# A four-layer graph kernel: the last layer opens with eight diagonal units, each beside one of the third layer's last eight tiles

## The chip, the cores and the metric

The kernel runs on one core of a Trainium2 chip. Its engines are TensorE (PE, matmuls), VectorE (DVE), ScalarE (ACT), GpSimd (POOL) and SyncE (SP, which here starts the transfers). Each works through its own queue in order and waits on semaphores for the others. The metric is the device time of one execution in microseconds (us), the median of several runs.

## The reference

Four graph layers on 4096 nodes with 64 features each share one 4096 x 4096 adjacency. After each layer the rows are normalised. The change touches the end of the third layer and the fourth.

```python
def _L0_gnn_ref(x, L, weight):             # layer 1: Chebyshev terms of L @ x
    ...
def _L1_gnn_ref(h, node_adj, edge_adj, ...):   # layer 2: attention and gates
    ...
def _L2_gnn_ref(input, adj, weight, bias):     # layer 3
    support = input @ weight
    mask = (adj != 0).astype(support.dtype)
    rank = jnp.cumsum(mask, axis=1)
    # at most the last 100 neighbours of a row count, each with a decay by its rank;
    # the decays times support are summed over the row
    ...
# layer 4 (curvature 1): pairs of nodes x, y, both moved with _expmap
sub = _mobius_add(-x, y, c)
sub_norm = jnp.maximum(jnp.linalg.norm(sub, axis=-1, keepdims=True), MIN_NORM)
2.0 / (sqrt_c * lam_x) * jnp.arctanh(arg) * sub / sub_norm   # _logmap
# the log maps are weighted by adj, summed over the neighbours and mapped back
```

The distance between two nodes is symmetric. So the fourth layer computes g, a factor made of the distance of a pair, once for both directions.

## The kernel before

**Third layer.** It works on 32 tiles of 512 x 1024 adjacency entries, `decayed(i)` on TensorE (L892 and L898, 16 matmuls of 512 columns). For each tile the rank codes come back from DRAM as bytes and are turned into decays in four blocks: two by ScalarE (L1287), one by VectorE (L1901), one by GpSimd (L615). Two buffers hold decays. The table `L2_TILES` gives the order; quarter Q of the nodes is done with its last tile. Then `copy_sums2`, `fold_sums`, `read_sums2`, `row_spread`, `root2` and `scale2` turn the sums of a quarter into normalised rows and the columns of U, the nodes' extended rows. `turn_nodes` transposes U, and `copy_nodes` puts it as UT and VT where the distances are computed from. `move_x` (L985) multiplies a quarter of the nodes with the layer's weights, `keep_moved` copies the result.

**Fourth layer.** It works on 80 units. A unit is one block of 128 nodes against a quarter of 1024 nodes. 32 units are on the diagonal of quarters (D, `own_units`), 48 off it (O, `off_units`). Per unit:
- TensorE: `distances` (L958), and, after VectorE's `multiply`, `push_apart` (L971);
- ScalarE: five passes over 128 x 1024: `raise_dist` (L1373), Ln (L1386), Exp (L1393), Exp (L1397), Ln (L1381);
- VectorE: `multiply` (L2015), the sum (L2099) and g (L2092); for O twice `mirror_weights` (L2025) as well;
- GpSimd: g times the edges (L635);
- TensorE: `gather` (L1012); for O also `turn_g` twice, four transposes each (L998), and per four O units, a quad, eight pairs of mirror products (L1027).

The order of every queue is written out by hand as a loop over "periods" n. TensorE's queue in period n is: push n, distances n+1, the second turn of g n-2, gather n-2, the mirror products that `products` plans for n (two behind two O units, otherwise one, three in the first quad), the first turn of g n-1. Distances n+1 wait for sum n-1, because two sets of PSUM banks alternate. The kind of each unit is set by the string "OODOD". `MOVED_AT`, `ROWS_AT`, `LAST_AT` and `POINTS_AT` say in which period the pieces of the third layer's end are done. Only tile 31 is still open when unit 0 has been pushed.

## Time and profile before

| | us |
|---|---|
| median of 3 runs | 1735.33 (1733.4 to 1735.41) |
| profiled execution | 1742.45, span 1740.6 |
| PE busy | 1542.5 |
| DVE busy | 1250.4 |
| ACT busy | 947.7 |
| POOL busy | 297.3 |

The span runs from the first to the last instruction of the profiled execution. Busy times are over the whole span; the stages have different limits, and the fourth layer is only the last 520 us of it. There ScalarE, which is 54% busy over the whole, is at nine tenths for most slices. The granted TensorE clock has a mean of 0.948 of full speed; it is low at the start of the fourth layer.

### The profile page before, as it was taken

The numbers are of one execution on the slowest core, as the hardware profiler recorded it, in microseconds if no ns is written. First come the engines' busy times: TensorE is split into PE (matmuls) and PEld (weight loads), VectorE is DVE, ScalarE is ACT, GpSimd is POOL, SyncE is SP. The second block draws the span as 40 slices with busy tenths as digits, with TensorE's granted clock in tenths as the row PEclk, the third lists the DMA queues.
The fourth block names the chain that finished last, engine by engine and source line by source line (L and its number), as shares of the span: only waits on it lengthen the run. The fifth ranks groups of instructions, "written<-read, shape, count | busy, mean of one in ns | idle before, by whom it ended". The sixth has DMA issues, their size and how long they took to land.

```text
span 1740.6 us, 21314 instructions
## 1 busy us (share of the span) xinstructions
PE 1542.5 (89%) x8169; PEld 653.1 (38%) x8214; DVE 1250.4 (72%) x1609; ACT 947.7 (54%) x920; POOL 297.3 (17%) x150
## 2 busy tenths in 40 slices
PE   6999989999999699999999997788788888888880
PEld 1433333333333344444444444233333333333330
DVE  4677699986888656747749654456567888888877
ACT  1233477753344433324343344656567999999964
POOL 1000000000000000000000002675224444444430
PEclk9999999999999799999999998999678999999995
DMA  9999599938999335333334302346124444544410
GB/s 349 412 413 413 213 357 381 392 130 316 413 413 381 115 146 193 147 146 146 145 135 156 145 1 73 121 133 218 37 97 133 148 155 136 186 163 158 136 46 24
DMA packets 118109, 348.99 MB, mean 201 GB/s; under 512 B 6324, under 2 KB 31224, under 8 KB 117752
## 3 DMA queue, kind: packets, MB, share of 16 engines
q1 hardware_dynamic: 106784, 329.27, 50.9%
q10 hardware_dynamic: 11224, 18.36, 2.8%
q8 instruction: 66, 1.08, 0.3%
q14 instruction: 35, 0.29, 0.1%
HBM read 329.78 MB, written 17.83 MB: 200 GB/s over the span
## 4 chain that ended last, share of the span: by engine, by line
PE 52%; issue 18%; DVE 13%; POOL 13%; ACT 2%; DMA 2%; SPq 0%; POOLq 0%; DVEq 0%; ACTq 0%
PE ps L741 13%; PE ps L863 13%; POOL ring L635 11%; PE ps L869 9%; DVE work L1611 4%; PE ps L674 3%; DVE work L1648 3%; PE ps L673 3%; PE ps L892 2%; POOL work L615 2%; PE ps L808 2%; DMA ring<-in_adjT 2%; PE ps L705 1%; PE ps L898 1%; DVE work L1624 1%
## 5 line engine op out<-in xcount | busy, mean ns | idle before, releaser
L615 POOL TENSOR_SCALAR work<-work 128x1024 int16<-128x1024 uint8 x32 | 97.0, 3041 | 1106.2 <-DMA work<-codes 1044.5
L863 PE MATMUL ps<-ring,X 128*64 128x512 f32 x512 | 264.0, 597 | 13.3 <-DVE ring L1867 13.3
L1134 ACT ACTIVATE work<-ps,code_bias 128x1024 uint8<-128x1024 f32 x128 | 135.8, 1111 | 247.7 <-PE ps L674 239.2
L864 PE MATMUL ps<-work,X 128*64 128x512 f32 x512 | 264.0, 597 | 0.0
L1255 ACT ACTIVATE work<-ring 128x2048 f32<-128x2048 f32 x64 | 122.2, 1911 | 222.0 <-PE ps L871 201.1
L635 POOL TENSOR_TENSOR ring<-ring,work 128x1024 f32<-128x1024 f32 x80 | 189.8, 2372 | 280.8 <-DVE work L2092 280.6
L871 PE MATMUL ps<-work 128*64 128x512 bf16 x768 | 208.2, 380 | 0.0
L869 PE MATMUL ps<-work 128*64 128x512 bf16 x768 | 208.2, 380 | 0.0
L958 PE MATMUL ps<-work 96*128 96x512 f32 x320 | 169.5, 655 | 0.0
L741 PE MATMUL ps<-ring,work 128*64 128x512 f32 x704 | 161.7, 601 | 0.0
L1864 DVE TENSOR_SCALAR work<-ring 128x2048 bf16<-128x2048 f32 x64 | 78.5, 1226 | 106.0 <-PE ps L871 105.8
L869 PEld LDWEIGHTS ps<-work 128*64 128x64 bf16 x768 | 84.8, 110 | 177.8 <-issue 152.3
L2099 DVE SCALAR_TENSOR_TENSOR work<-ps,work 128x1024 f32<-128x1024 f32 x80 | 97.9, 1224 | 46.5 <-ACT work L1393 34.4
L1638 DVE TENSOR_TENSOR work<-work 128x512 bf16<-128x512 bf16 x248 | 105.4, 425 | 33.3 <-DVE work L1611 12.9
L1867 DVE TENSOR_SCALAR ring<-ring 128x2048 f32<-128x2048 f32 x64 | 78.1, 1220 | 40.7 <-ACT work L1255 40.7
L1611 DVE TENSOR_TENSOR work<-work,ring 128x1024 f32<-128x1024 f32 x85 | 103.5, 1218 | 0.7
L741 PE MATMUL ps<-ring,X 128*64 128x512 f32 x352 | 88.0, 646 | 16.5 <-DMA ring<-in_adjT 16.5
L674 PE MATMUL ps<-work,minus_ones 128*128 128x512 bf16 x256 | 98.0, 383 | 4.7 <-DVE Y L1591 2.5
L892 PE MATMUL ps<-work 128*128 128x512 bf16 x243 | 67.0, 416 | 29.6 <-ACT work L1287 13.3
L1012 PE MATMUL ps<-ring 128*64 128x512 f32 x320 | 89.3, 637 | 2.9 <-POOL ring L635 2.9
L863 PEld LDWEIGHTS ps<-ring,X 128*64 128x64 f32 x512 | 68.9, 137 | 55.7 <-issue 16.0
L1287 ACT ACTIVATE work<-work 128x2048 int16<-128x2048 uint8 (+1 forms) x32 | 67.5, 2119 | 39.0 <-PE ps L898 36.6
(316 smaller groups left out, 2766.0 us busy)
## 6 DMA issues: line engine op xcount, KB each, us to landing
ring<-in_adjT SPq DMA_DIRECT2D x90, 2048.0 KB, 10.6
work<-in_adjT SPq DMA_DIRECT2D x26, 2048.0 KB, 12.0
ring<-in_adjT SPq DMA_DIRECT2D x48, 1024.0 KB, 7.7
codes<-work ACTq DMA_DIRECT2D x64, 256.0 KB, 6.1
work<-codes SPq DMA_DIRECT2D x32, 512.0 KB, 3.6
ring<-in_adjT SPq DMA_DIRECT2D x32, 512.0 KB, 3.6
X<-in_x ACTq DMA_DIRECT2D x1, 1024.0 KB, 6.9
work<-in_xT SPq DMA_DIRECT2D x2, 512.0 KB, 22.6
```

Source lines behind the costliest of these rows:

```text
L615: nc.gpsimd.tensor_scalar(decay[i % 2][:, 3, :].rearrange("p (h c) -> p h c", h=2), code_in[:, i % RING, :, 3, :], 128.0, None, ALU.mult). ...
L635: nc.gpsimd.tensor_tensor(u.edges, u.edges, u.angle, ALU.mult).then_inc(weighted, 1)
L674: mm = nc.tensor.matmul(ps[:, bank, :], minus_ones[:], later[:, u, j, :], start=False, stop=True)
L741: mm = nc.tensor.matmul(ps[i * F:(i + 1) * F, a.banks + h, :], rows_of(a, k), a.room[:, k, cols], start=start, stop=stop)
L863: nc.tensor.matmul(ps[0:F, h, :], rows, ring[:, r, k, cols], start=start, stop=stop)
L864: nc.tensor.matmul(ps[F:P, h, :], rows, negs[:, pair, i, cols], start=start, stop=stop)
L869: nc.tensor.matmul(ps[0:F, 2 + h, :], part, more[:, pair, i, cols], start=start and t == 0, stop=stop and t == 2)
L871: mm = nc.tensor.matmul(ps[F:P, 2 + h, :], part, less[:, pair, i, cols], start=start and t == 0, stop=stop and t == 2)
L958: mm = nc.tensor.matmul(ps[:, u.banks + h, :], UT[:, u.rows * P:(u.rows + 1) * P], VT[:, cols], start=True, stop=True)
L1134: nc.scalar.activation(codes[:, u, k:k + 2, :].rearrange("p k c -> p (k c)"), ps[:, bank:bank + 2, :].rearrange("p k c -> p (k c)"), ACT.Relu,
L1255: nc.scalar.activation(negs[:, pair], ring[:, s % RING, 2 * pair:2 * pair + 2, :], ACT.Relu, scale=-1.0).then_inc(negs_made, 1)
L1611: ins = V.tensor_tensor(row_sum[:, a.q, :], row_sum[:, a.q, :], edges, ALU.add)
```

## The change

The unit order becomes eight D, then 22 times OOD, then OOOODD. `JOINT = 8`, and `BEFORE = SLOTS - JOINT` is 24: unit 0's distances are put in front of tile 24, and period n holds tile 25+n behind distances n+1. The decays of these tiles are made inside the periods by all three engines. Of the nodes only quarter 0 is turned as a whole before the units; quarters 1, 2 and 3 follow as halves (`turn_half`, `copy_half`, `copy_signs`) in the periods that `HALVES_AT` names. GpSimd copies their signs, which ScalarE did for quarters 1 and 2. Rows are scaled in four groups, one for each quarter, and no longer in three. `move_x` moves from periods 2, 3, 4, 10 to 10, 11, 12, 16. The first units' angles and edges get other places in the ring, loaded between code tiles 11 and 12.

```diff
-        sums2_in = [turn_in[:]] * 3 + [x_moved_words[:, 0:QC]]
+        sums2_in = [turn_in[:], turn_in[:], x_moved_words[:, QC:2 * QC], x_moved_words[:, 0:QC]]
...
+        JOINT = 8
...
-                self.angle = angles[:, n % 3, :]
+                self.angle = ring[:, 3, n % 3, :] if n < JOINT else angles[:, n % 3, :]
...
-        for five in range(UNITS // 5):
-            for kind in "OODOD" if five < UNITS // 5 - 1 else "OOODD":
...
+        for kind in "D" * JOINT + "OOD" * 22 + "OOOODD":
...
+        AHEAD = 7
+        for u in own_units[0:AHEAD]:
+            u.edges = (ring[:, 2, 0, :], ring[:, 2, 1, :], ring[:, 2, 2, :], ring[:, 2, 3, :], ring[:, 1, 0, :],
+                       ring[:, 1, 1, :], ring[:, 3, 3, :])[u.place]
...
-        COPIED = (1, 2, 3, 5)
-        MOVED_AT = (2, 3, 4, 10)
-        ROWS_AT = 4
-        LAST_AT = 6
-        POINTS_AT = [1, 8, 11]
+        COPIED = (1, 3, 5, 7)
+        SIGNED = (2, 6, 10, 14)
+        HALVES_AT = {3: (1, 0), 4: (1, 1), 7: (2, 0), 8: (2, 1), 14: (3, 0), 15: (3, 1)}
+        HALF_BANKS = (None, 4, 4, 7)
+        MOVED_AT = (10, 11, 12, 16)
+        ROWS_AT = 10
+        POINTS_AT = [6, 9, 14]
...
-        SUM_AT, READ_AT, SPREAD_AT = (15, 17, 25), (17, 19, 27), (18, 20, 28)
-        TURN_AT, OUT_AT = (22, 23, 30), (24, 25)
+        SUM_AT, READ_AT, SPREAD_AT = (15, 17), (17, 21), (18, 22)
+        ROOT_AT, SCALE_AT, OUT_AT = 19, 20, 22
...
-        GROUPS = ((0, 1), (2,), (3,))
-        ROOT_AT, SCALE_AT = (21, 29), (22, 30)
+        BEFORE = SLOTS - JOINT
...
+            for i in range(BEFORE + 3):
+                make_decays(i)
             for u in units:
+                if BEFORE + 3 + u.n < SLOTS:
+                    make_decays(BEFORE + 3 + u.n)
                 pool.wait_ge(g_made, u.n + 1)
...
+            def turn_half(n, h):
+
+                pe.wait_ge(ext_ready, n + 1)
+                wait_for_copies(COPIED[n - 1] + h)
+                if h == 0 and n == 1:
+                    pe.wait_ge(sum2_read, 3)
+                if h == 0 and n == 3:
+                    pe.wait_ge(moved_kept, 3)
                 for c in range(GB):
...
+            for i in range(12, BEFORE + 1):
+                if i == BEFORE:
+                    distances(units[0])
                 decayed(i)
...
             for n in range(LAST_PERIOD):
+                if n in HALVES_AT:
+                    turn_half(*HALVES_AT[n])
                 if unit_at(n):
                     push_apart(units[n])
                 if unit_at(n + 1):
                     distances(units[n + 1])
+                if BEFORE + 1 + n < SLOTS:
+                    decayed(BEFORE + 1 + n)
...
-                if n == 0:
-                    decayed(SLOTS - 1)
                 if n == 1:
-                    fold_sums(NQ - 1)
+                    fold_sums(2)
+                if n == JOINT:
+                    fold_sums(3)
...
+            def copy_half(n, h):
+
+                act.wait_ge(vt_copied, COPIED[n - 1] + h + 1)
...
                 if n == 0:
-                    copy_sums2(NQ - 1)
+                    copy_sums2(2)
                 if n == 1:
-                    copy_nodes(2)
-                    read_sums2(NQ - 1)
+                    scale2(1)
                 if n == 2:
-                    row_spread(2, NQ - 1)
+                    read_sums2(2)
                 if n == 3:
+                    row_spread(2, 2)
+                if n == 5:
+                    scale2(2)
+                if n == JOINT - 1:
+                    copy_sums2(3)
+                if n == JOINT:
                     dve.wait_ge(decay_used, SLOTS)
                     V.memset(aggT[:], 0.0).then_inc(sums_cleared, 1)
-                if n == 5:
-                    scale2(2)
+                if n == 9:
+                    read_sums2(3)
+                if n == 10:
+                    row_spread(2, 3)
+                if n == 12:
+                    scale2(3)
```

The first place is TensorE's queue where the units begin. Before, this is period 0 with tile 31 (L892, L898), between push (L971) and distances (L958) of units 0, 1 and 2:

```order
L971 MATMUL ps<-work 128x512 [waits prod_made,signs_copied]
L971 MATMUL ps<-work 128x512
L958 MATMUL ps<-work 128x512 x2
L892 MATMUL ps<-work 128x512 [waits decay_pool,decay_dve,decay_act,part2_made2]
L892 MATMUL ps<-work 128x512 x7
L898 MATMUL ps<-work 64x512 x8
L971 MATMUL ps<-work 128x512 [waits prod_made]
L971 MATMUL ps<-work 128x512
L958 MATMUL ps<-work 128x512 [waits vt_tail_copied,sum_made,vt_copied,ut_copied]
L958 MATMUL ps<-work 128x512
```

Now it is the end of period 2 and period 3: a gather (L1041), half of quarter 1's nodes turned (L962), push (L1000), distances (L989), a tile (L920, L926) and the next gather:

```order
L1041 MATMUL ps<-ring 64x512 [waits sum2_copied,points_made,weighted]
L1041 MATMUL ps<-ring 64x512
L962 MATMUL ps<-ident,work 128x128 [waits vt_tail_copied,vt_copied,sum2_read,ut_copied,ext_ready]
L962 MATMUL ps<-ident,work 128x128 x3
L1000 MATMUL ps<-work 128x512 [waits prod_made]
L1000 MATMUL ps<-work 128x512
L989 MATMUL ps<-work 128x512 [waits sum_made]
L989 MATMUL ps<-work 128x512
L920 MATMUL ps<-work 128x512 [waits decay_pool,decay_dve,decay_act,part2_made2]
L920 MATMUL ps<-work 128x512 x7
L926 MATMUL ps<-work 64x512 x8
L1041 MATMUL ps<-ring 64x512 [waits points_made,weighted]
```

A tile stands behind the distances in seven periods, where it stood in one, and the turn of half a quarter stands in front of a push.

The second place is VectorE's queue in period 10 of the new kernel, behind the points: the sum of the first eight units (L2075), g 9 (L2125), mirror multiplies (L2058), sum 10 (L2132), multiply 11 (L2048), the end of the spread (L1858 to L1860) and the norm of rows (L1558):

```order
L2075 TENSOR_TENSOR work<-work,ps 128x512 [waits sums_cleared,gathered]
L2125 SCALAR_TENSOR_TENSOR work<-work,stage_words 128x1024 [waits inv_made,angle_made]
L2058 TENSOR_TENSOR work<-ps,ring 128x4x128 [waits strip_in0,g_turned]
L2132 SCALAR_TENSOR_TENSOR work<-ps,work 128x1024 [waits far_added,root_made]
L2048 SCALAR_TENSOR_TENSOR turn_in<-ps,turn_in 128x1024 [waits raised]
L1858 TENSOR_TENSOR room_f<-Y 128x512
L1859 TENSOR_REDUCE stats<-room_f 128x8 [waits row_steps2]
L1860 TENSOR_SCALAR stats<-stats 128x8 [waits row_steps2]
L1558 TENSOR_TENSOR X<-Y,stats 128x512
L2058 TENSOR_TENSOR work<-ps,ring 128x4x128 [waits g_turned]
```

Before, the same pieces stood in period 2, where there was no sum of units to add yet and no norm of rows:

```order
L2092 SCALAR_TENSOR_TENSOR work<-work 128x1024 [waits inv_made,angle_made]
L2025 TENSOR_TENSOR work<-ps,ring 128x4x128 [waits strip_in0,g_turned]
L2099 SCALAR_TENSOR_TENSOR work<-ps,work 128x1024 [waits far_added,root_made]
L2015 SCALAR_TENSOR_TENSOR stage_words<-ps,stage_words 128x1024 [waits raised]
L1822 TENSOR_TENSOR room_f<-Y 128x512
L1823 TENSOR_REDUCE stats<-room_f 128x8 [waits row_steps2]
L1824 TENSOR_SCALAR stats<-stats 128x8 [waits row_steps2]
L2025 TENSOR_TENSOR work<-ps,ring 128x4x128 [waits g_turned]
L2092 SCALAR_TENSOR_TENSOR work<-work,turn_in 128x1024 [waits inv_made,angle_made]
```

The last mirror multiply of the pair, which the next turn of g and move_x wait for, has two instructions more ahead of it, and the spread's two halves are one period apart as they were.

## Rows read from the trace of the kernel before

**Rows 1.** Windows, start-up and rhythm: length, busy us (count) by engine, clock, DMA.

```profile
1215.00:1358.00 143.00, 116.13 (x403) 53.28 (x404) 97.51 (x131) 96.35 (x102) 45.39 (x21) 0.79 0.29 94
1358.00:1680.00 322.00, 285.59 (x1206) 114.41 (x1206) 268.89 (x271) 297.80 (x306) 144.89 (x61) 1.00 0.46 150
```

**Rows 2.** Source view of L971: duration min/median/max, first and last start.

```profile
L971 PE MATMUL ps<-work x160: 371/380/629, 1215.0 to 1680.3; 3*128 3x512 bf16 x160
```

**Rows 3.** Timeline of one cycle: start, us, engine, instructions [idle before <- releaser].

```profile
1421.32 0.60 PE L971 MATMUL ps<-work 3*128 3x512 bf16 x2 [0.59 <-DVE stage_words L2015]
...
1426.22 0.60 PE L971 MATMUL ps<-work 3*128 3x512 bf16 x2 [0.51 <-DVE work L2015]
...
1431.35 0.60 PE L971 MATMUL ps<-work 3*128 3x512 bf16 x2 [0.58 <-DVE turn_in L2015]
...
1431.88 1.98 PE L958 MATMUL ps<-work 96*128 96x512 f32 x4
...
1434.98 1.21 DVE L2015 SCALAR_TENSOR_TENSOR stage_words<-ps,stage_words 128x1024 f32<-128x1024 f32 x1
...
1436.93 0.63 PE L998 MATMUL ps<-ident,work 128*128 128x128 f32 x4 [0.76 <-DVE work L2025]
...
1437.49 0.60 PE L971 MATMUL ps<-work 3*128 3x512 bf16 x2
...
1440.04 1.02 ACT L1373 ACTIVATE work<-ps 128x1024 f32<-128x1024 f32 x1 [1.10 <-PE ps L958]
```

**Rows 4.** Timeline of PE: last tiles and start-up.

```profile
1135.10 3.59 PE L892 MATMUL ps<-work 128*128 128x512 bf16 x8 [5.99 <-ACT work L1245]
...
1183.78 1.67 PE L892 MATMUL ps<-work 128*128 128x512 bf16 x7
...
1234.56 1.11 PE L998 MATMUL ps<-ident,work 128*128 128x128 f32 x4 [5.65 <-DVE work L2025]
...
1240.35 3.68 PE L985 MATMUL ps<-w_sb,work 64*128 64x64 f32 x16
...
1244.92 3.78 PE L958 MATMUL ps<-work 96*128 96x512 f32 x4
...
1265.68 3.20 PE L985 MATMUL ps<-w_sb,work 64*128 64x64 f32 x16 [1.61 <-DVE work L2057]
...
1302.59 0.60 PE L971 MATMUL ps<-work 3*128 3x512 bf16 x2 [0.21 <-DVE stage_words L2015]
...
1358.60 0.60 PE L971 MATMUL ps<-work 3*128 3x512 bf16 x2
```

**Rows 5.** Timeline of DVE: scalings and reading of sums.

```profile
1205.77 0.99 DVE L1928 SCALAR_TENSOR_TENSOR stats<-stats 128x8 f32<-128x8 f32 x1
...
1212.47 0.69 DVE L1948 TENSOR_TENSOR work<-Y,stats 128x512 f32<-128x512 f32 x1
...
1227.32 0.67 DVE L1965 TENSOR_TENSOR Y<-ps,Y 128x512 f32<-128x512 f32 x1
...
1229.67 0.69 DVE L1815 TENSOR_TENSOR Y<-Y,stats 128x512 f32<-128x512 f32 x1
...
1275.79 0.16 DVE L1928 SCALAR_TENSOR_TENSOR stats<-stats 128x8 f32<-128x8 f32 x1
...
1279.51 0.69 DVE L1948 TENSOR_TENSOR work<-Y,stats 128x512 f32<-128x512 f32 x1
```

**Rows 6.** Timeline of ACT: decays of a tile, copy of half a quarter.

```profile
1204.79 1.91 ACT L1287 ACTIVATE work<-work 128x2048 int16<-128x2048 uint8 x1 [0.56 <-PE ps L898]
...
1293.75 0.59 ACT L1364 ACTIVATE work<-ps 96x512 f32<-96x512 f32 x1 [1.54 <-DVE work L1960]
```

**Rows 7.** Page, costliest groups: count | busy us, mean ns | idle before.

```profile
L615 POOL TENSOR_SCALAR work<-work 128x1024 int16<-128x1024 uint8 x32 | 97.0, 3041 | 1106.2 <-DMA work<-codes 1044.5
...
L635 POOL TENSOR_TENSOR ring<-ring,work 128x1024 f32<-128x1024 f32 x80 | 189.8, 2372 | 280.8 <-DVE work L2092 280.6
```

More of the change, by code:

```diff
@@ L213, in adjacency_stack @@
         units, off_units, own_units = [], [], []
-        for five in range(UNITS // 5):
-            for kind in "OODOD" if five < UNITS // 5 - 1 else "OOODD":
-                left, stream = (off_left, off_units) if kind == "O" else (own_left, own_units)
-                u = Unit(len(units), *left.pop(0))
-                u.place = len(stream)
-                stream.append(u)
-                units.append(u)
+        for kind in "D" * JOINT + "OOD" * 22 + "OOOODD":
+            left, stream = (off_left, off_units) if kind == "O" else (own_left, own_units)
+            u = Unit(len(units), *left.pop(0))
+            u.place = len(stream)
+            stream.append(u)
+            units.append(u)
+        assert len(units) == UNITS
         for stream in (off_units, own_units):
@@ L392, in adjacency_stack @@
         edges_in = [[sem(f"edges_in{i}_{r}") for r in range(2)] for i in range(2)]
+        first_edges_in = [sem(f"first_edges_in{i}") for i in range(AHEAD)]
         strip_in = [sem(f"strip_in{r}") for r in range(2)]
@@ L532, in load_own @@
                     "p a b c -> p (a b c)")
-                sp.dma_start(u.edges, src).then_inc(edges_in[1][u.place % 2], 16)
+                sp.dma_start(u.edges, src).then_inc(
+                    first_edges_in[u.place] if u.place < AHEAD else edges_in[1][u.place % 2], 16)
             def load_strip(quad):
@@ L542, in load_strip @@
                     sp.dma_start(strip_part(quad, t), src).then_inc(strip_in[quad % 2], 16)
-            sp.wait_ge(pair_used, 2 + 2 * (SLOTS - RING + 2))
-            for u in own_units[0:2]:
+            for i in range(12):
+                load_codes(i)
+            for u in own_units[0:AHEAD]:
                 load_own(u)
@@ L548, in _ @@
                 load_off(u)
[L549 to L552 removed]
+            for i in range(12, SLOTS):
+                load_codes(i)
+            turns = [(own_units[i - 2].n + 1, 0, i) for i in range(AHEAD, len(own_units))]
+            turns += [(4, 3, 0), (AHEAD, 4, 1)]
             turns += [(off_units[i - 3].n + 1, 1, i) for i in range(4, len(off_units), 2)]
@@ L561, in _ @@
                     load_off(off_units[i])
+                if kind >= 3:
+                    sp.wait_ge(gathered, done)
+                if kind == 4:
+                    sp.wait_ge(weighted, JOINT)
+                if kind >= 3:
+                    load_strip(i)
                 if kind == 2:
@@ L607, in _, with make_decays @@
             pool.sem_inc(consts_made, 1)
-            for i in range(SLOTS):
+            def make_decays(i):
                 pool.wait_ge(code_loaded[i % RING], (i // RING + 1) * 16)
@@ L1350, in _ @@
             part2(3, 2)
-            for i in range(14, SLOTS):
+            for i in range(14, BEFORE + 2):
                 make_decays(i)
@@ L1996, in _ @@
             rest2(3, 1)
-            for i in range(14, SLOTS):
+            for i in range(14, BEFORE + 2):
                 make_decays(i)
```

174 lines of the change are left out of this document (84 added, 90 removed).

## The prediction

> **How the profile was read.** First the windows view, which cuts the run's end into stages. From the first push (the matmuls of L971, the first own step of a unit) at 1215.0 us, the last layer takes 143 us to reach push 18 and then 322 us to push 79 [rows 1, 2, 4]. In the second stretch ScalarE is busy 297.8 of 322 us at full TensorE clock, so it nearly sets the pace; in the first no engine is full (TensorE 116, ScalarE 96 of 143 us) and the granted clock is 0.79 [rows 1]. So the end of the run is 18 units of start-up, 61 units of rhythm, and a tail after the last push that the change leaves alone.
>
> Then the timeline of one cycle of the rhythm. I call "period n" the time from push n to push n+1. TensorE's work in it depends on whether units n-1 and n-2 are off the diagonal (O) or on it (D), since only O units have transposes (turn_g) and mirror products. The pushes at 1421.32, 1426.22, 1431.35 and 1437.49 give 4.90 us for a period behind D and O, 5.13 behind O and D, and 6.14 behind two O [rows 3]. In the last one TensorE does 8 transposes and two mirror products; it waits 0.76 us for VectorE's mirror multiply, pushes late, and ScalarE then sits 1.10 us until the distances come [rows 3]. Nothing gives this back.
>
> Last the start-up. Extra TensorE and VectorE pieces (move_x, the sums' folding and reading, scaling, the nodes' copies) stand in the period's chain. After a wait of 5.65 us for a VectorE multiply, move_x takes 3.68 us and a unit's distances 3.78 us against 1.98 us in the rhythm; that is 1.2 GHz against 2.4. A wait of only 1.61 us is again followed by a slow move_x (3.20 us) [rows 3, 4].
>
> The sum is made on the profiled execution (1742.45 us, span 1740.6), and its difference is put on the median of the runs, 1735.33, which lies 7.1 us lower.
>
> **Rhythm (units 18 to 79).** The order changes from OODOD to OOD. Periods 18 to 78 are 61. Before: 13 behind two O, 24 behind O and D, 24 behind D and O: 13 x 6.14 + 24 x 5.13 + 24 x 4.90 = 320.5 us; measured 1680.3 - 1358.6 = 321.7 [rows 2, 4], so 1.2 us are left over for starts of a quad. Now two D lead out and OOD has one pair of O in three: 22 behind two O (19 in the cycles, 3 in the closing OOOODD), 20 and 19 of the others: 22 x 6.14 + 20 x 5.13 + 19 x 4.90 = 330.8, with the same 1.2 it is 332.0. **Cost +10.3 us.** Each kind of period in this sum occurs in the old cycle beside the same neighbours, and the planner gives each the same number of mirror products (two behind two O, else one), so I take it as it stands. Bounds: +5 if a pair's delay is partly hidden by ScalarE's slack, +14 if the three pairs in a row at the end add to each other.
>
> **Entry.** Tile 24 starts at 1183.78; its first matmuls (seven records) take 1.67 us [rows 4], the whole some 2.7. Until there the new order has one turn of nodes fewer on TensorE, and the scaling is for one quarter; but the first scaling still holds up a turn. I leave tile 24 where it was. Push 0 comes behind it: the raised distances (1.02 us) and the multiply (1.21 us) [rows 3] go on beside the tile, and ScalarE has two decay instructions (1.91 us each) [rows 6] in front. I get 4.8 us, so push 0 at 1188.6, 26.4 us earlier than before.
>
> **Periods 0 to 7, beside tiles 25 to 31.** ScalarE has 297.8/61 = 4.9 us for a unit [rows 1] and 1.9 for a tile's decays, so 6.8 us; TensorE has a tile (2.7), distances, push and gather, 6.2 us; GpSimd 3.04 + 2.37 = 5.4 us [rows 7]. The floor is 6.8, set by ScalarE. On top comes what stands in the chain, laid out by hand in the order of each queue:
> - 0: no Ln yet, 5.3. 1: copy_sums2 and root2, 7.6.
> - 2: scale2(1) is in VectorE's queue ahead of g 1, sum 2, multiply 3 and read_sums2, and turn_half(1,0) waits for the sums read. TensorE has about 4 us with nothing and holds push 3 back: 11.3.
> - 3: the clock is low after this gap: distances 3.8, the tile slower; VectorE's decays and row_spread stand ahead of copy_half, ScalarE's two copies (0.59 each, [rows 6]) behind it, and turn_half(1,1) behind these: 12.5. 4: gap before it again: 9.8.
> - 5: 6.4. 6: scale2(2) again ahead of multiply 7: 8.0. 7: copy_sums2 and copy_half before turn_half(2,1): 8.5.
> Together 69.4, so push 8 at 1258. Before, push 8 is at 1302.6 [rows 4]: a lead of 44.6 us, at the widest.
>
> The second and the third scaling of before (19 instructions, L1928 to L1948) show both prices: 7.4 us with GpSimd running beside it, 4.4 us with it idle [rows 5]. I take 4.7 in periods 1 and 5, since GpSimd then waits for g. The Trainium skill (GPSIMD Engine Reference, section 8. Key points) says that GpSimd shares its SBUF interfaces with VectorE and contends with instructions of two SBUF inputs or in a 2-port mode. The two durations agree; by the rule alone both scalings would run beside decays in this stage, at 7.4 us, and the sum would be 5 to 6 us higher.
>
> **Periods 8 to 17.** Nearly everything that before stood in periods 1 to 10 beside units 1 to 10 now stands here beside units 8 to 17:
> - 8: turn_half(2,1), fold_sums(3), aggT cleared: 8.4. 9: 7.6.
> - 10: VectorE's queue is read_sums2 (3.0 us, from 1227.32 to 1230.36 [rows 5]), points, the sum of the first eight units, g 9, a mirror multiply, sum 10, multiply 11, spread, norm rows, and only then the mirror multiply that turn_g 9 waits for; behind it move_x(0) at 3.7 us: 16.2.
> - 11: distances 3.8, raise, multiply, norm, keep_moved, move_x(1): 12.1. 12: the same with scale2(3) in front of keep_moved: 16.2.
> - 13 and 14: turn_half(3,0) and (3,1) behind keep_moved and the copies: 11.5 and 10.8. 15: 6.5. 16: move_x(3): 8.5. 17: 5.2.
> Together 103.0: push 18 at 1361.0, 2.4 us later than before. The 44.6 us of lead are given back, since the ten periods cost about twice those of the rhythm. DMA is not in the sum: 5.5 MB of edges are issued between code tiles 11 and 12, where TensorE waits 5.99 us for another copy anyway [rows 4], and each ring place is loaded again as many units ahead as before. The new waits on copied signs and half nodes are in the terms above; what is queued behind them is push n.
>
> Bounds of the start-up: if every stretch that I put at 1.2 GHz ran at 2.4, seven periods lose 2.3 us each on distances and push, six turns 0.4, three move_x 1.8: -24 us. If both scalings run beside GpSimd and tile and unit are slow in all eight joint periods, about +14 us.
>
> **Sum:** +2.4 + 10.3 = +12.7 us: 1755 for the profiled execution, **1748 us** for the median.
>
> **Rivals.**
> - A, the lead is kept (faster). Mechanism: in periods 2 to 8 the tiles' matmuls lie between distances and gather and keep TensorE at 2.4 GHz, so move_x and distances run at 1.98 instead of 3.8 us. -24 + 12.7 gives -11: 1724 us. For it: granted clock near full in most of the tile stage. Against it: here a wait of 1.61 us was enough. It decides if push 18 comes before 1345. Chance 0.18. The skill (TensorE: Matmul & The Clock Gate, section Loop structure matters more than you think) says that matmuls which follow each other at once hold the clock while VectorE copies; by this rule the joint stage would be such a loop, and the time would be this rival's.
> - B, the rhythm is not slower: the 6.14 us belong to something in the five-cycle that three-cycles lack. Then +2.4: 1738 us. Against it: the wait for the mirror multiply comes with the two O before it, always. Chance 0.13.
> - C, the joint stage costs more: GpSimd's decays for tile 27+n are queued behind weighting n-1, which waits for g, and VectorE's scalings run beside it; 2 us in each of eight periods: +29, 1764 us. For it: in the tile stage of before TensorE already waits for GpSimd's decays. Against: 5.4 us fit into 8. Chance 0.19.
> - Forecast, 0.50, own range 1740 to 1757.
>
> **The numbers.** A change under 0.2% (3.5 us) can't be told from none. Faster: A and a little of the forecast's lower edge, 0.20. Same: most of B and a little of the forecast, 0.13. Slower: the rest, 0.67. The range 1727 to 1763 reaches to near A and takes most of C.
>
> **What will show it.** Right: periods of 6.14 us once in three units at a granted clock of 1.00, 16.2 us a cycle; push 0 near 1189, push 8 near 1258, push 18 near 1361; GpSimd, ScalarE and VectorE none full in the start-up; long periods 2, 3, 10, 11, 12. Wrong: a cycle under 15.9 us; a granted clock over 0.9 between push 8 and push 18; or push 8 later than 1270 with TensorE waiting for L635's decays (C).

## The result and the profile after

The changed kernel takes 1756.92 us (median of 4 runs, 1753.96 to 1760.57), the kernel before 1735.04 beside it: a ratio of 1.0129 with an interval of 1.0105 to 1.0153, or 22 us slower. The forecast was 1748, slower, with a range of 1727 to 1763. The direction holds, the time is inside the range, and of the 22 us the forecast had 12.7.

The profiled execution of the changed kernel took 1754.72 us (span 1753.0). A second profile of the unchanged kernel (the first experiment) took 1735.18 (span 1733.4), 7.3 us less than the one that the forecast was made from. It is the fairer one to compare with. The stages, from the pushes (L971 before, L1000 after):

| us | push 0 at | pushes 0 to 18 | pushes 18 to 79 | tail | span |
|---|---|---|---|---|---|
| before, as in the rows | 1215.0 | 143.5 | 321.5 | 60.5 | 1740.6 |
| before, profiled again | 1211.6 | 139.7 | 321.5 | 60.6 | 1733.4 |
| after | 1184.6 | 178.4 | 331.4 | 58.7 | 1753.0 |
| after less before again | -27.0 | +38.7 | +9.9 | -1.9 | +19.6 |

Windows of the kernel after, for the joint stage (pushes 0 to 8), units 8 to 17 and the rhythm; the columns are the window, its length, busy us by engine (count), the granted clock, the DMA share and GB/s. They answer to [rows 1].

```profile
1184.60:1254.80 70.20, 59.66 (x217) 22.67 (x218) 48.55 (x85) 55.75 (x59) 36.99 (x17) 0.81 0.17 56
1254.80:1363.00 108.20, 83.12 (x238) 38.99 (x238) 62.29 (x92) 52.97 (x58) 32.12 (x18) 0.65 0.24 78
1363.00:1694.30 331.30, 294.42 (x1290) 122.18 (x1290) 276.06 (x282) 299.21 (x307) 144.69 (x61) 1.00 0.46 153
```

The same view of the kernel before, profiled again:

```profile
1211.60:1291.60 80.00, 61.16 (x193) 29.86 (x193) 49.87 (x73) 44.82 (x49) 16.49 (x7) 0.70 0.16 51
1291.60:1351.30 59.70, 52.65 (x218) 21.68 (x218) 48.13 (x58) 52.23 (x54) 28.95 (x14) 0.94 0.49 159
1351.30:1672.80 321.50, 285.09 (x1203) 113.97 (x1203) 268.43 (x271) 297.27 (x306) 144.94 (x61) 1.00 0.46 150
```

Single profiles of one stage differ by some us, and the experiments show by how much. In the eight profiles of the changed kernel and its variants push 0 lies between 1182.9 and 1190.0, though their edits touch nothing ahead of it but one instruction that makes zeros. Experiment 3 leaves the first 18 periods of the changed kernel as they are too, and they take 174.7 us there, with 67.1 for pushes 0 to 8 at a granted clock of 0.89. So a difference of 3 or 4 us between two profiles of the start-up shows nothing by itself.

TensorE's first two windows add up to 142.8 busy of 178.4 us after and 113.8 of 139.7 before: 29.0 more busy and 9.7 more idle. Seven tiles stand in the stretch where one stood (tile 31, behind push 0), so six have come into it. Their matmuls (L920 and L926; before, L892 and L898) are busy for 24.1 us after and 2.9 before: 21 us more, of which six tiles are 16 at the forecast's own estimate of 2.7 us each at full clock. The distances of the 18 units take 11 us more with the same instructions (54.6 and 43.4), since of them 11 took over 2.5 us after (most 3.78, full clock 1.98), and 5 before. I call these slow distances from here on. The turns, gathers and mirror products differ by smaller amounts of either sign. So the 27 us by which the units start earlier are spent on the tiles brought with them, on half clock and on waits, and more comes on top.

The rhythm, in the timeline of PE (start, us, engine, instructions, idle before and its releaser); it answers to [rows 3]:

```profile
1422.43 0.63 PE L1026 MATMUL ps<-ident,work 128*128 128x128 f32 x4 [0.77 <-DVE work L2058]
1422.98 0.60 PE L1000 MATMUL ps<-work 3*128 3x512 bf16 x2
...
1427.88 0.60 PE L1000 MATMUL ps<-work 3*128 3x512 bf16 x2 [0.50 <-DVE stage_words L2048]
...
1433.02 0.60 PE L1000 MATMUL ps<-work 3*128 3x512 bf16 x2 [0.60 <-DVE work L2048]
...
1438.61 0.63 PE L1026 MATMUL ps<-ident,work 128*128 128x128 f32 x4 [0.76 <-DVE work L2058]
1439.17 0.60 PE L1000 MATMUL ps<-work 3*128 3x512 bf16 x2
```

4.90, 5.14 and 6.15 us, a cycle of 16.2; the wait of 0.76 for VectorE's mirror multiply stands ahead of the late push, as before. The waits view sums it up: 22 such waits, where the order has 22 pairs.

```profile
PE ps L1026 <- DVE work L2058: 16.3, 22, 0.8
PE ps L1000 <- DVE work L2048: 11.6, 19, 0.7
PE ps L1000 <- DVE stage_words L2048: 9.7, 19, 0.7
```

Two pieces of the start-up. PE in periods 10 and 16 of the kernel after, which answers to [rows 4]:

```profile
1282.53 1.09 PE L1026 MATMUL ps<-ident,work 128*128 128x128 f32 x4 [2.05 <-DVE work L2058]
1283.55 3.67 PE L1013 MATMUL ps<-w_sb,work 64*128 64x64 f32 x16
...
1345.81 0.66 PE L1026 MATMUL ps<-ident,work 128*128 128x128 f32 x4 [2.24 <-DVE Y L2058]
1346.39 1.22 PE L1041 MATMUL ps<-ring 128*64 128x512 f32 x4
1351.23 1.09 PE L1026 MATMUL ps<-ident,work 128*128 128x128 f32 x4 [3.62 <-DVE work L2058]
1352.24 3.67 PE L1013 MATMUL ps<-w_sb,work 64*128 64x64 f32 x16
1355.85 1.03 PE L1000 MATMUL ps<-work 3*128 3x512 bf16 x2
1356.81 3.78 PE L989 MATMUL ps<-work 96*128 96x512 f32 x4
```

And DVE in period 16, which opens with push 16 at 1341.06:

```profile
1347.16 1.22 DVE L2048 SCALAR_TENSOR_TENSOR turn_in<-ps,turn_in 128x1024 f32<-128x1024 f32 x1
1348.29 0.17 DVE L2104 TENSOR_SCALAR stats<-edge_sum 128x32 f32<-128x32 f32 x1
...
1350.31 0.18 DVE L2110 TENSOR_SCALAR stats<-stats 128x32 f32<-128x32 f32 x1
1350.40 0.68 DVE L2058 TENSOR_TENSOR work<-ps,ring 128x512 f32<-128x512 f32 x1
```

Here TensorE has its transposes to do, but the mirror multiply that frees their bank (L2058, 1350.40) stands on VectorE behind the multiply for the next unit (1.22 us) and the seven small steps of `make_scales` (2.1 us). TensorE waits 3.62 us, and then move_x and the distances run at 1.2 GHz (3.67 and 3.78 us).

### The profile page after: what moved, and what is told of

The parts are those of the page before. It is cut to its first block, busy times and chain, and to the rows that moved or that the text cites. A ratio compares the mean times of both kernels' runs of the same rounds, so it can differ in the third digit from the quotient of the medians.

```text
span 1753.0 us, 21412 instructions
## 1 busy us (share of the span) xinstructions
PE 1553.8 (89%) x8214; PEld 657.1 (37%) x8214; DVE 1252.9 (71%) x1629; ACT 945.9 (54%) x922; POOL 304.7 (17%) x158
## 4 chain that ended last, share of the span: by engine, by line
PE 58%; DVE 21%; ACT 14%; issue 4%; DMA 2%; POOL 1%; SPq 0%; DVEq 0%; ACTq 0%; POOLq 0%
PE ps L769 13%; PE ps L891 12%; PE ps L897 9%; PE ps L989 5%; DVE work L1647 4%; DVE work L1684 4%; PE ps L701 3%; PE ps L702 3%; ACT work L1412 2%; PE ps L836 2%; DVE work L2132 2%; DMA ring<-in_adjT 2%; ACT stage_words L1404 1%; ACT work L1424 1%; ACT work L1404 1%
## 5 line engine op out<-in xcount | busy, mean ns | idle before, releaser
L891 PE MATMUL ps<-ring,X 128*64 128x512 f32 x512 | 263.9, 597 | 13.3 <-DVE ring L1903 13.3
L892 PE MATMUL ps<-work,X 128*64 128x512 f32 x512 | 263.9, 597 | 0.0
L663 POOL TENSOR_TENSOR ring<-ring,work 128x1024 f32<-128x1024 f32 x72 | 170.6, 2370 | 264.0 <-DVE work L2125 264.0
L989 PE MATMUL ps<-work 96*128 96x512 f32 x320 | 177.5, 681 | 0.2 <-ACT work L1350 0.2
L1674 DVE TENSOR_TENSOR work<-work 128x512 bf16<-128x512 bf16 x248 | 105.5, 425 | 33.3 <-DVE work L1647 12.9
L2132 DVE SCALAR_TENSOR_TENSOR work<-ps,work 128x1024 f32<-128x1024 f32 x72 | 88.2, 1225 | 43.7 <-ACT work L1424 28.9
L701 PE MATMUL ps<-work,later_or_self 128*128 128x512 bf16 x256 | 98.6, 385 | 2.1 <-issue 2.1
L769 PE MATMUL ps<-ring,X 128*64 128x512 f32 x352 | 84.1, 621 | 18.0 <-DMA ring<-in_adjT 18.0
L920 PE MATMUL ps<-work 128*128 128x512 bf16 x256 | 70.4, 424 | 24.2 <-ACT work L1318 9.3
L1041 PE MATMUL ps<-ring 128*64 128x512 f32 x320 | 91.5, 652 | 0.0
L1026 PE MATMUL ps<-ident,work 128*128 128x128 f32 x384 | 63.6, 290 | 30.4 <-DVE work L2058 26.4
## 6 DMA issues: line engine op xcount, KB each, us to landing
ring<-in_adjT SPq DMA_DIRECT2D x90, 2048.0 KB, 10.9
work<-in_adjT SPq DMA_DIRECT2D x26, 2048.0 KB, 11.9
```

The lines of the kernel that those rows point to most:

```text
L663: nc.gpsimd.tensor_tensor(u.edges, u.edges, u.angle, ALU.mult).then_inc(weighted, 1)
L701: nc.tensor.matmul(ps[:, bank, :], later_or_self[:], mask[:, u, k, :], start=True, stop=False)
L769: mm = nc.tensor.matmul(ps[i * F:(i + 1) * F, a.banks + h, :], rows_of(a, k), a.room[:, k, cols], start=start, stop=stop)
L891: nc.tensor.matmul(ps[0:F, h, :], rows, ring[:, r, k, cols], start=start, stop=stop)
L892: nc.tensor.matmul(ps[F:P, h, :], rows, negs[:, pair, i, cols], start=start, stop=stop)
L989: mm = nc.tensor.matmul(ps[:, u.banks + h, :], UT[:, u.rows * P:(u.rows + 1) * P], VT[:, cols], start=True, stop=True)
```

## Experiments

Each is told against the kernel before, timed beside it (1735.0 to 1735.4 us), with the stages of one profile. Where a kernel is named "changed", the edit stands on the changed kernel. "Mirror multiply" is VectorE's `mirror_weights`, "mirror products" are TensorE's matmuls for a quad; the later expectations call the first a mirror product too, and the multiply for the next unit a product.

**1. The kernel before again** (no edit).

> The kernel before, unchanged, profiled once more. Its first profiled execution took 1742.45 us, its timed runs 1733.4 to 1735.4. Theory: these 7 us are start-up (stretches of TensorE at half clock that fall differently from run to run), so the new profile shows a start-up (push 0 to push 18) between 136 and 144 us and a rhythm (push 18 to 79) of 321 to 322 us; ratio of the timed runs 1.000. Rival: being profiled costs 7 us everywhere; then the new profile is again at 1742 with a start-up of 143.5 us.

1735.16 us, ratio 1.0002 (0.9986 to 1.0017). The profile is the second row of the table above: push 0 3.4 us earlier and pushes 0 to 18 3.8 us shorter than in the profile of the forecast, all the rest within 0.1. The first profile's surplus over the median lay in two places: ahead of the units (tile 24 starts at 1180.1 here and at 1183.8 there) and in the start-up, which the change rebuilds. It is no cost of profiling: the ten timed runs of this same kernel lie between 1731.72 and 1743.29.

**2. The changed kernel, mirror multiply first behind two O units.**

```diff
+                two_off = off_at(n - 1) and off_at(n - 2)
+                if two_off:
+                    mirror_weights(units[n - 2], 1)
                 if unit_at(n + 1):
                     multiply(units[n + 1])
...
-                if off_at(n - 2):
+                if off_at(n - 2) and not two_off:
                     mirror_weights(units[n - 2], 1)
```

> The changed kernel; in periods behind two off-diagonal units VectorE does the second mirror multiply ahead of the next unit's multiply. Theory (the 6.14 us of such a period are set by VectorE's mirror multiply standing behind the multiply, and TensorE's transposes waiting for it): these periods shrink to 5.4 to 5.6 us, 22 of them, 12 to 15 us in all, push 18 to 79 in 317 to 320 us. Rival (TensorE's own work of such a period sets it): under 3 us, periods stay at 6.0 or more.

1728.33 us, ratio 0.9966 (0.9953 to 0.998): 28.6 us below the changed kernel. Pushes 18 to 79 take 316.8 us, 14.6 less. The period behind two O units is 5.50 us, and the wait ahead of its turn is gone:

```profile
1401.44 0.60 PE L1000 MATMUL ps<-work 3*128 3x512 bf16 x2 [0.59 <-DVE work L2048]
...
1406.20 0.66 PE L1026 MATMUL ps<-ident,work 128*128 128x128 f32 x4
1406.94 0.60 PE L1000 MATMUL ps<-work 3*128 3x512 bf16 x2
```

Pushes 0 to 18 lose 12.1 us as well (166.3), though the edit was meant for the rhythm. Of these 9.0 stand in pushes 8 to 18: the units 8 to 17 hold pairs of O too, and there the queue ahead of that multiply is longer still. The other 3.0 stand in pushes 0 to 8, where every unit is D and the edit changes nothing; they are the difference between two profiles.

**3. The changed kernel, TensorE's mirror products of quads dealt out the other way round**: one behind two O units, two elsewhere.

```diff
-                room = len(left) if end == quad_ends[-1] else 3 if quad == 0 else 2 if turns == 2 else 1
+                room = len(left) if end == quad_ends[-1] else 3 if quad == 0 else 1 if turns == 2 else 2
```

> The changed kernel; behind two off-diagonal units one mirror product is planned and otherwise two, where it was two and one. Theory (VectorE's mirror multiply sets the 6.14 us): TensorE only waits longer for it, the periods stay at 6.1 to 6.2, time within 2 us. Rival (TensorE's work sets it): the long periods fall to about 5.7 us and the time by about 9 us.

1773.74 us, ratio 1.0235 (1.0217 to 1.0254). Both expectations miss. With less TensorE work the period behind two O stays at 6.1 us, so that period belongs to VectorE, as the theory had it; but pushes 18 to 79 grow to 348.3 us. The cause is in rows of PE from there:

```profile
1404.47 0.63 PE L1026 MATMUL ps<-ident,work 128*128 128x128 f32 x4 [1.19 <-DVE work L2058]
1405.03 0.60 PE L1000 MATMUL ps<-work 3*128 3x512 bf16 x2
1405.56 3.50 PE L989 MATMUL ps<-work 96*128 96x512 f32 x4
...
1411.44 0.60 PE L1000 MATMUL ps<-work 3*128 3x512 bf16 x2 [0.76 <-DVE stage_words L2048]
```

```profile
PE ps L1026 <- DVE work L2058: 25.1, 22, 1.2
```

The mirror product taken out of the period is TensorE work that stood in front of the wait, which is now 1.2 us long instead of 0.76. In the next period distances take up to 3.50 us instead of 1.98, and the period 6.4 instead of 4.9. Of the 61 distances of the rhythm, 13 take over 2.5 us, each of them the first behind such a wait; their surplus over 1.98 adds up to 14 of the 17 us. In the changed kernel none does. The granted clock of the rhythm is 0.94 here and 1.00 there. Two products in a short period cost nothing by themselves: the 7 such periods without a slow distance still take 4.89.

**4. The changed kernel, what others wait for first**: `keep_moved`, the second mirror multiply and the nodes' halves right behind the multiply for the next unit, ahead of scaling, norms and points.

```diff
                 if BEFORE + 2 + n < SLOTS:
                     make_decays(BEFORE + 2 + n)
+                if n - 1 in MOVED_AT:
+                    keep_moved(MOVED_AT.index(n - 1))
+                if off_at(n - 2):
+                    mirror_weights(units[n - 2], 1)
+                if n in HALVES_AT:
+                    copy_half(*HALVES_AT[n])
                 if n == 0:
                     copy_sums2(2)
```

> The changed kernel; on VectorE keep_moved, the second mirror multiply and copy_half stand ahead of the third layer's remaining pieces (reading, spread, scaling, norm, scales) in each period. Theory (the start-up's long periods are TensorE waiting for these three behind the pieces): period 10 goes from 15.7 to about 13 us, 12 from 16.3 to about 12, 16 from 14.8 to 10 or 11; push 0 to 18 falls by 9 to 13 us, the rhythm stays at 331. Rival (the half clock alone makes these periods long): less than 4 us.

1735.38 us, ratio 0.9998 (0.9985 to 1.0011), 21.5 us below the changed kernel, all of it in pushes 0 to 18: 156.0 instead of 178.4; the rhythm stays at 331.2. More than expected, above all in period 12, which falls to 8.1 us and not to 12 (periods 10 and 16: 13.6 and 10.1). Its windows for pushes 0 to 8 and 8 to 18:

```profile
1189.00:1254.00 65.00, 53.74 (x216) 21.03 (x216) 48.04 (x84) 55.24 (x59) 37.40 (x17) 0.91 0.19 61
1254.00:1345.00 91.00, 79.15 (x238) 34.15 (x238) 62.04 (x92) 53.33 (x58) 32.14 (x18) 0.67 0.28 93
```

TensorE's idle time falls from 35.6 to 23.1 us, which is the 9 to 13 us of the expectation, and its busy time from 142.8 to 132.9 with the same instructions: less of it at half clock. Against the start-up of experiment 3 (33.3 idle, 141.4 busy) the gains are 10.2 and 8.5. Either way a wait costs its own length here, and then something near the same again.

**5. The kernel before with the edit of 2.**

> The kernel before (units in the order O O D O D) with one move in VectorE's loop: where units n-1 and n-2 are both off the diagonal, the second mirror product of unit n-2 stands ahead of the product of unit n+1 instead of behind it, as in the second experiment. Theory (TensorE's wait for that product makes the period behind two O units 0.6 us longer, in either order): the kernel before has 13 such periods where the changed one has 22, so its units 18 to 79 fall from 321.5 to 312-315 us, and the total by 7 to 11 us, to 1724-1728. Rival (only the new order has that queue to pay for): no change within 3 us. If the theory holds, the changed order keeps some 3 to 4 us of its cost in units 18 to 79 even with the move (316.8 measured there).

1726.38 us, ratio 0.9944 (0.9928 to 0.996). Pushes 18 to 79 take 313.5 us, 8.0 less, for 13 pairs (0.6 each); in the changed kernel 14.6 for 22 (0.66 each). The theory holds in both orders.

**6. The kernel before with the new order of units only.**

```diff
-        for five in range(UNITS // 5):
-            for kind in "OODOD" if five < UNITS // 5 - 1 else "OOODD":
...
+        for kind in "D" * 8 + "OOD" * 22 + "OOOODD":
```

> The kernel before with nothing but the new order of units: eight D first, then OOD 22 times, then OOOODD; the third layer's last tiles stay ahead of unit 0. Theory (the order alone costs 10 us in the later units, since each cycle of three has a period behind two O): units 18 to 79 at 330-332 us instead of 321.5; the first 18 units, of which eight are D and take no mirror work, get 5 to 12 us shorter than the 139.7 of the kernel before; total -3 to +6 us against it. Then the joint stage and what it spreads over the first 18 periods answer for the rest of the 20 us. Rival (the loss comes with the joint stage, the order is harmless): units 18 to 79 at 320-324 us and the total 5 to 15 us below the kernel before.

1738.6 us, ratio 1.0023 (1.0008 to 1.0037). The rhythm is 332.2 us, which is the changed kernel's: the 10 us belong to the order. The first 18 periods gained less than expected, 2.2 us (137.5). So the order answers for some 3 of the 22 us, and the joint stage, with the new places of the third layer's pieces, for some 18. That is a difference; the joint stage in the old order of units was not run. Against this kernel the changed one starts its units 23.6 us earlier and needs 40.9 us more for the first 18.

**7. The changed kernel, `make_scales` in period 32.**

```diff
-                if n == POINTS_AT[-1] + 2:
+                if n == 32:
                     make_scales()
```

> The changed kernel with make_scales (seven steps of VectorE, each waiting for the one before, 2.1 us in all) in period 32 instead of period 16. Theory (in period 16 they keep the mirror product that TensorE waits for, its two waits of 2.2 and 3.6 us are followed by TensorE at half clock): period 16 falls from 14.8 to 8-11 us, period 32 grows by 0 to 2.5 us; total 3 to 6 us below the changed kernel, 1751-1754 where it has 1757. Rival (period 16 is long by the move of x and the turned halves that stand in it, whatever VectorE does): period 16 stays above 13.5 and the total within 2 us or up to 2 us longer by period 32.

1754.83 us (1748.01 to 1760.37), ratio 1.0106 (1.0073 to 1.0139). In the profile period 16 falls from 14.8 to 10.4 us (it takes 13.2 in experiment 3, which changes nothing there) and period 33 grows by 0.8. The mechanism is as expected; the total is 2 us lower, less than the 3 to 6 expected, and the intervals of the two kernels overlap, so that the gain in the total stays open. The profiled execution is the fastest of the four (1748.01).

**8. The changed kernel with matmuls of zeros in TensorE's waits.** They add zero to PSUM banks that are free just then.

```diff
+            KEPT_BUSY = {2: (12, 5), 3: (10, 5), 6: (7, 5), 7: (12, 5), 10: (8, 4), 11: (7, 4), 12: (20, 4), 13: (12, 4),
+                         14: (7, 4), 16: (16, 4)}
+
+            def keep_busy(n):
+
+                times, bank = KEPT_BUSY[n]
+                for _ in range(times):
+                    nc.tensor.matmul(ps[:, bank, :].rearrange("p (a c) -> p a c", a=2), zeros[:, 0:P],
+                                     zeros[:].unsqueeze(1).broadcast_to([P, 2, HALF // 2]), start=False, stop=False,
+                                     skip_group_check=True)
...
+                if n in KEPT_BUSY and n not in (11, 12):
+                    keep_busy(n)
                 if off_at(n - 1):
                     turn_g(units[n - 1], 0)
+                if n in (11, 12):
+                    keep_busy(n)
```

> The changed kernel with idle matmuls of zeros on TensorE (bf16, 128 x 512, added to banks of PSUM that are free to be added zero, 7 to 20 of them) ahead of the pieces that wait longest, in periods 2, 3, 6, 7, 10 to 14 and 16 of the last layer. They change no value; they fill TensorE's waits. Theory (the long periods are long because TensorE's clock stands at half after waits of 1.6 to 5 us, so that work bound by TensorE takes twice its time): the granted clock between push 0 and push 18 rises from 0.71 to over 0.9, the periods 2, 3, 10, 11, 12, 13 and 16 lose 2 to 3 us each, push 0 to push 18 falls from 178 to 155-165 us and the total by 12 to 22. Rival (the waits themselves, behind VectorE and ScalarE, make up the long periods and the clock only follows them): the clock rises, but the stretch keeps 172 us or more, or grows by the added matmuls where they run past their wait.

1739.63 us, ratio 1.0017 (1.0004 to 1.0031): 17.3 us less than the changed kernel, with 111 matmuls more and the one instruction that makes the zeros. Pushes 0 to 18 take 160.1 us. Windows of this kernel for pushes 0 to 8 and 8 to 18, against 0.81 and 0.65 without the zeros:

```profile
1190.00:1256.00 66.00, 60.82 (x257) 24.00 (x257) 49.42 (x84) 55.17 (x58) 37.89 (x17) 0.95 0.19 61
1256.00:1350.00 94.00, 86.48 (x308) 38.34 (x306) 62.23 (x91) 53.31 (x59) 31.94 (x18) 0.78 0.27 90
```

The rows of the longest one (20 zeros, period 12): they fill the gap to within 2.00 us, and move_x behind them takes 2.00 instead of 3.67 us.

```profile
1301.85 4.48 PE L1071 MATMUL ps<-zeros 128*128 128x512 bf16 x20
1308.33 2.00 PE L1015 MATMUL ps<-w_sb,work 64*128 64x64 f32 x16 [2.00 <-DVE work L2107]
```

The rival falls: the clock is not a mere follower of the waits, since filling them, with every other instruction in its place, returned 17 us. With 0.78 in the second window some of the clock's cost is still there. Two details of the expectation miss: the clock stays below 0.9 over the whole stretch (slow distances go from 11 to 7), and only four periods lose 2 us or more (12: 3.9, 7: 2.3, 14: 2.2, 16: 2.1).

**9 and 10. All three moves** (2, 4 and 7) in the changed kernel, and as far as they fit in the kernel before (there the copies of the last nodes and, up to period 8, the mirror multiplies that are not behind two O units keep their place).

> The changed kernel with the three moves in VectorE's loop together: the mirror product ahead of the next unit's product behind two O units, the pieces that TensorE and GpSimd wait for (keep_moved, mirror products, halves of the nodes) right behind the product, and make_scales in period 32. Alone they measured 14.6 us less in units 18 to 79 with 12 in units 0 to 18 (first), 22 us less in units 0 to 18 (second), 6 us (third). Theory (the first's later part adds to the second and third, which overlap in the start-up): push 0 to push 18 at 148-156 us, units 18 to 79 at 316-319, total 1713-1722. Rival (the pieces only trade places, each gain in the start-up was the same one): total 1722-1729.

> The kernel before with the same three moves as far as its order of work allows: the mirror product ahead of the product behind two O units, keep_moved and from unit 9 on the mirror products right behind the product, make_scales in period 32. Theory: units 18 to 79 at 312-315 us as with the first move alone (313.5), the start-up at 128-136 us (136.0 with the first move alone, whose TensorE waits in periods 2, 3 and 4 stand for decays and copies that these moves don't touch): total 1719-1726. Rival (its start-up gains as much as the changed kernel's, 20 us): total 1705-1712. If the changed kernel with the three moves comes within 3 us of this one, the joint stage itself costs nothing more than what VectorE's order took.

Changed kernel: 1717.64 us, ratio 0.9903 (0.9886 to 0.9919); pushes 0 to 18 at 153.1, 18 to 79 at 320.9. Kernel before: 1719.29, ratio 0.9907 (0.989 to 0.9923); 126.6 and 314.1. Both totals are as expected; the start-up of the kernel before is shorter than expected (128 to 136), and the rhythm of the changed kernel longer (316 to 319). The two kernels are level: the moves give the changed kernel 39 us and the kernel before 16. So what the changed kernel lost on the kernel before went with VectorE's order of work, and by these totals the joint stage as such neither costs nor gains: it starts 28.9 us earlier and needs 26.5 us more to push 18. Its rhythm is 4 us longer than in experiment 2, in periods 33 and 34 alone; the last section shows the rows. The profiled execution is the slowest of the four (1722.52), so this need not be so in every one.

**11 and 12. The three moves and the zeros**, in both (92 matmuls of zeros in the changed kernel, 44 in the kernel before).

> The changed kernel with the three moves in VectorE's loop and the matmuls of zeros on TensorE (here 5 to 12 of them, since the waits are shorter). Theory (waits and clock are two parts of the same cost, so the zeros give back less than their 17 us beside a start-up that has already lost 25): push 0 to push 18 at 140-147 us instead of 153.1, total 1705-1712. Rival (the three moves have taken what the zeros took): 1715-1719.

> The kernel before with the same three moves and with matmuls of zeros in periods 2, 4, 6, 7 and 8. Theory: its first 18 periods fall from 126.6 to 118-124 us (its longest wait, 5.6 us ahead of the turn in period 2, and three of 1.5 to 3.7 us get company), total 1711-1717. Rival (its half clock costs little, since the long periods there wait for VectorE): within 2 us of 1719. Between this one and the changed kernel with the same additions stands what the order and the joint stage are worth by themselves: 5 us either way.

Changed kernel: 1707.28 us (1706.8 to 1713.85), ratio 0.9842 (0.9818 to 0.9866), 28 us below the kernel before and the fastest of all. Pushes 0 to 18 take 143.7 us, two distances are slow, and the windows show clocks of 0.97 and 0.87:

```profile
1184.30:1246.30 62.00, 58.28 (x253) 23.23 (x253) 48.99 (x84) 55.17 (x58) 37.60 (x17) 0.97 0.19 63
1246.30:1328.10 81.80, 72.90 (x294) 32.65 (x293) 60.36 (x85) 53.60 (x59) 32.87 (x18) 0.87 0.31 103
```

Kernel before: 1722.04 us, ratio 0.9918 (0.9899 to 0.9938), where 1711 to 1717 were expected. That is 2.7 us more than without the zeros, by medians whose intervals overlap: no gain, and a loss that isn't shown. In the profile pushes 0 to 18 take 132.5 us (126.6 without, 118 to 124 expected), and period 2 17.8 us where it took 14.4. The zeros of period 2 were put where TensorE had no wait; the wait of 5.64 us stands two steps earlier, and they run at their own cost:

```profile
1229.85 1.11 PE L1000 MATMUL ps<-ident,work 128*128 128x128 f32 x4 [5.64 <-DVE work L2039]
1230.89 1.98 PE L1014 MATMUL ps<-ring 128*64 128x512 f32 x4
1232.80 4.45 PE L1049 MATMUL ps<-zeros 128*128 128x512 bf16 x16
1237.09 0.60 PE L1000 MATMUL ps<-ident,work 128*128 128x128 f32 x4
```

Whether zeros in the right place would help there was not tried. So the 15 us between the two kernels here are not what order and joint stage are worth, for which 5 us either way were expected; without the zeros that is nothing clear of noise (experiments 9 and 10).

## Why the prediction was right or wrong

The sum was +2.4 for the start-up and +10.3 for the rhythm. Against the kernel before profiled again the start-up measured +11.7 (push 18 at 1363.0 and 1351.3) and the rhythm +9.9. So the mechanism of the rhythm and its size were right, and the start-up was priced 9.3 us too low.

**Rhythm, +10.3: right.** Measured +9.9, 16.2 us a cycle, 6.15 us once in three, 22 waits. Shown by experiments 2, 5 and 6: it is the queue in front of VectorE's mirror multiply, it comes with each pair of O, and the order alone brings it. Rival B falls.

**Entry, push 0 at 1188.6: 4 us too late** (1184.6). Of this 3.4 us are the profile's: in the profile of before again push 0 is at 1211.6, and 26.4 less than that is 1185.2. Tile 24, from which the forecast counts, starts at 1180.5 after and at 1180.1 in that profile, so it did stay where it was.

**Periods 0 to 7, 69.4: right** (70.1), in the single ones to within 1.8 us (10.3, 11.7, 9.4 for periods 2 to 4, forecast 11.3, 12.5, 9.8; 10.3 for period 7, forecast 8.5), with misses of either sign that cancel. The floor of 6.8 us is not one: period 5 took 6.0, and ScalarE was busy 55.8 of 70.2 us.

**The lead at push 8 was misread.** The push at 1302.59 in the rows of before is push 9. Push 8 stands eight periods behind the 1215.0 of push 0:

```profile
1295.47 1.03 PE L971 MATMUL ps<-work 3*128 3x512 bf16 x2
```

So the lead that the forecast calls 44.6 us is 37.5 by its own numbers, and it measured 36.8 (1291.6 less 1254.8). The sum does not use it: it compares push 18 with push 18.

The scaling of quarter 1 takes the short price, 4.5 us:

```profile
1198.34 0.15 DVE L1964 SCALAR_TENSOR_TENSOR stats<-stats 128x8 f32<-128x8 f32 x1
...
1202.20 0.69 DVE L1982 TENSOR_TENSOR work<-Y,stats 128x512 f32<-128x512 f32 x1
```

GpSimd's decays of 2.77 us had ended 1.3 us into it, and the steps beside them took 0.15 to 0.17 us like those behind them. The rule on shared interfaces (the Trainium skill, GPSIMD Engine Reference, section 8. Key points) is neither borne out nor refuted by this, since the two hardly met. Rival C falls too: GpSimd is busy 37 of the stage's 70 us, and TensorE's waits there (11.9 us in all) are for VectorE and ScalarE.

**Periods 8 to 17, 103.0: 5.2 short** (108.2). The mis-sized term is "16: move_x(3): 8.5", measured 14.8. It left out the seven steps of `make_scales`, which the moved points bring into period 16, ahead of the multiply that TensorE waits for, and the half clock behind the wait. Periods 10 to 13 came out at 15.7, 11.5, 16.3 and 10.9 (forecast 16.2, 12.1, 16.2, 11.5). Experiment 7 took 4.4 us off period 16 in its profile; what remains over the forecast there, 1.9 us in period 16 and 1.0 in period 17, stays open.

**The last step of the sum went wrong as well**: "its difference is put on the median of the runs, 1735.33, which lies 7.1 us lower". The forecast for the profiled execution, 1755, came out (1754.72), and the median did not follow (1748 forecast, 1756.92 measured). That the first came out is partly luck: the units started 4.0 us sooner than forecast and the tail was 1.8 shorter, and periods 8 to 17 took 5.2 more. The profile of before lay above its median because of its entry (3.4 us) and start-up (3.8). The 172.4 us of the new start-up were laid out by hand from single pieces, not carried over from that stretch, so its 3.8 us of surplus were hardly in them to be taken off. That is an argument, and no run tests it. With the stages of the second profile the same terms give 1211.6 - 26.4 + 69.4 + 103.0 + 321.5 + 10.3 + 60.6 + 1.8 (launch, 1735.18 less 1733.4) = 1751.8. Of the 8.9 us between forecast and median, then, 3.8 are that subtraction, 2.9 are the sum's own (5.2 too little for periods 8 to 17, some 2 too much in the tail), and 2.2 the profiled run's distance below its own median. Each of these is of the size by which single profiles differ.

**Rival A, the clock stays high, falls**: 0.81 beside the tiles (0.89 in three variants that run the same instructions there, experiments 2, 3 and 7) and 0.65 after them. The rule that matmuls which follow each other at once hold the clock (the Trainium skill, TensorE: Matmul & The Clock Gate, section Loop structure matters more than you think) agrees with experiment 8, where filled waits brought the clock from 0.65 to 0.78. But the joint stage is no such loop: TensorE is busy 59.7 of 70.2 us in it and waits for ScalarE and VectorE. Its -24 us for full clock were never reached; the zeros, which brought the clock of the 18 periods from 0.71 to 0.85, returned 17.

**One reading of before was incomplete.** "After a wait of 5.65 us" move_x took 3.68 us, but a second wait of 1.75 stood right ahead of it. In experiment 10 the wait of 5.64 is there and the second is gone, and move_x takes 2.29.

## What to carry to other kernels

A wait on TensorE is priced with the work behind it, which may run at half clock; take it away by putting what TensorE waits for ahead of VectorE's other work, and only then fill what is left with idle matmuls, at the wait itself and nowhere else. When two stages are put beside each other, list every small piece that the moved steps bring into each period, the ones nobody waits for too. And before a difference is carried from a profile to the median, find out in which stage the profile's surplus lies: in a stage that the change rebuilds it must not be subtracted. Where single profiles of one stage differ by 4 us, no term of the sum is known better than that.

## What the runs showed of the hardware

The clock does not depend on the length of a wait alone. With 22 waits of 0.76 us in the rhythm no distance was slow; with 22, of which 20 are 1.18 to 1.22 us (experiment 3), 13 of 61 were. Each of the 13 is the first behind one of these 20 waits (2.56 to 3.50 us); behind the other 7 the first distances took 1.98 or 1.99. And one wait of the same length had both ends. In experiment 9, ahead of push 34, with `make_scales` in period 32:

```profile
1423.67 0.59 PE L1000 MATMUL ps<-work 3*128 3x512 bf16 x2 [1.56 <-DVE work L2048]
1424.19 3.68 PE L989 MATMUL ps<-work 96*128 96x512 f32 x4
```

In experiment 11, at the same push:

```profile
1412.27 0.59 PE L1002 MATMUL ps<-work 3*128 3x512 bf16 x2 [1.57 <-DVE work L2065]
1412.79 1.98 PE L991 MATMUL ps<-work 96*128 96x512 f32 x4
```

The period took 8.7 us in the one and 5.3 in the other. TensorE's instructions of the 84 us ahead of this push are the same in both, at the same distances from it to 0.02 us. Yet the granted clock falls to half at 1424.3 in the first and does not fall in the second. What decides between them these runs don't show.
